# Two attention blocks with feed-forward layers on one core: the experts' weight loads grouped behind two key transposes instead of four

## The chip, the core and the metric

The kernel runs on one core of one Trainium2 chip. The metric is the device time of one execution in microseconds. Five engines work side by side: TensorE (PE, with its weight loads PEld), VectorE (DVE), ScalarE (ACT), GpSimd (POOL) and SyncE (SP), which here does nothing but issue transfers; 16 DMA engines carry them out. All semaphores and orders are written by hand.

## The reference, cut to what matters

Eight batches of 128 tokens with 128 features pass two layers. Each layer is cross-attention with 16 heads of 8 features against a shared context, followed by a feed-forward part: a quantized gated one in layer 0, eight experts with the best two mixed in layer 1.

```python
x = x + L0_xattn(layernorm(x), ctx, ctx, mask_per_batch, Wq, Wk, Wv, Wo)   # 16 heads of 8, softmax over 128 keys
x = x + L0_ffn(layernorm(x), w_gate, w_up, w_down)                         # quantized activations and weights, silu
x = x + L1_xattn(layernorm(x), ctx, ctx, shared_mask, Wq, Wk, Wv, Wo, bo)
h = relu(einsum('td,ehd->eth', xt, W1) + b1)       # the experts: E = 8, hidden 256
y = einsum('eth,eoh->eto', h, W2) + b2
out = einsum('eto,te->to', y, comb)                # comb: softmax weights of the top 2 experts
```

W1 and W2 are the experts' weights: 8 x 256 x 128 numbers of 4 bytes each, 1 MB apiece. They are used in the last part of layer 1 alone.

## The kernel before

A unit is one layer of one batch; there are 16, numbered n = 0 to 15 in the order of `UNIT_ORDER` (line 76). n = 0 to 6 are layer 0 of batches 0 to 6, n = 7 is layer 1 of batch 0, n = 8 layer 0 of batch 7. Each unit is a chain of named steps: `kv` (keys and values), `ks` (the key transpose), `q`, `max` (a first product of queries and keys for the row maxima, four parts), `qb`, `exp` (the shifted scores, four parts), `pv`, `oT`, `aT`, `wo`, and then in layer 0 the feed-forward steps `xq`, `fxT`, `gate`, `th`, `z1`, `up`, `hT`, `down`, or in layer 1 the router and the expert steps `z` and `y`.

A planner (`plan`, line 303) runs on the host before the kernel is built. It turns costs, due times and biases into one fixed order of steps for each engine; the engines then run these orders strictly, with a semaphore wait ahead of each step. The planner knows the key transposes but not the loads that are issued between them, so its orders are the same whatever loads stand there.

The keys of a unit are put by ScalarE and GpSimd into `kst`, a bf16 tile of 128 x 2048, and SyncE turns them by a DMA transpose (step `ks`, line 617) into `kblk`, which has five slots. TensorE reads `kblk` first in step `max` (lines 761 and 763: a mask matmul, then the products) and again in `exp` (line 779). `max` of n = 6 waits for the transpose of n = 6. In TensorE's order around it stand: qb of n = 4, the last part of max of n = 5, the first part of max of n = 6, exp of n = 4, fxT of batch 0, aT of n = 2, exp, the second part of max of n = 6, exp, gate of batch 0, fxT of batch 1, wo of n = 2, exp, up of batch 0, pv of n = 3. In VectorE's order z1 of batch 0 (line 1262) comes after wo of n = 2; it reads the tanh that ScalarE (line 1039) makes of the gate matmul.

SyncE issues all loads of the later phases between its transposes: after the transpose of unit n it calls `later_loads(n)` (line 578). For n = 1 these are two mask loads and half of the context. For n = 5 they begin with three small ones (b1, gT, gb). The tiles w1_sb and w2_sb are filled in four parts of four chunks each, every part two transfers of 256 KB (128 rows of 2 KB), part k behind the transpose of n = 5 + k. All eleven transfers count up one semaphore, s_moe, to 176; the logit and `z` steps of layer 1, batch 0, wait for that full count.

SyncE's order is: ks of n = 0 to 8, qs of n = 7, ks of n = 9 and so on. Each ks waits for GpSimd's last step on the keys of its unit and for the transpose two before it. All transfers issued by SyncE go through one hardware queue.

Of the kernel before, what the change touches and what calls it, by code (L numbers as in the profile page):

```python
# [378 lines left out]
def build(nc, x, ctxT, mask0, mask0T, mask1, mask1T, w0q, w0kv, w0o, w1q, w1kv, w1o, bo,  # L379
# [17 lines left out]
    with ExitStack() as ctx:  # L397
        def sb(name, shape, dt=F32):
            return ctx.enter_context(nc.sbuf_tensor(name, shape, dt))

        def sem(name):
            return ctx.enter_context(nc.semaphore(name))
# [9 lines left out]
        def after(eng, step, u, i=None):  # L412

            eng.wait_ge(done[step], u * counts[step] + (counts[step] if i is None else i + 1))
# [11 lines left out]
        def wait_landed(eng, n, name="ks"):  # L426
            eng.wait_ge(landed[name][n % 2], 16 * (n // 2 + 1))
# [24 lines left out]
        w1_sb = sb("w1_sb", [P, ZCH, P])  # L452
        w2_sb = sb("w2_sb", [P, ZCH, P])
# [64 lines left out]
        s_cst, s_x0, s_x, s_ctx0, s_ctx, s_wq, s_wkv, s_w1, s_wo, s_b2, s_moe = [sem(n + "_in") for n in (  # L518
            "cst", "x0", "x", "ctx0", "ctx", "w0q", "w0kv", "w1", "w0o", "b2", "moe")]
# [48 lines left out]
        @block.sync  # L568
        def _(sp):
            sp.dma_start(x_sb[:, 0, :], x[0]).then_inc(s_x0, 16)  # L570
            sp.dma_start(cst_sb[:, :], cst).then_inc(s_cst, 16)
            sp.dma_start(x_sb[:, 1:4, :], x[1:4].rearrange("b t d -> t b d")).then_inc(s_x, 16)
            def masks(part, first, last):
                sp.dma_start(m0_i[:, first:last, :], mask0[first:last].rearrange("b q k -> q b k")
                             ).then_inc(s_mask[2 * part], 16)
                sp.dma_start(m0T_i[:, first:last, :], mask0T[:, first:last, :]).then_inc(s_mask[2 * part + 1], 16)

            def later_loads(n):

                if n == 0:  # L580
                    masks(1, 1, 2)
                    sp.dma_start(wo_sb[0][:, :], w0o).then_inc(s_wo, 16)
                    sp.dma_start(x_sb[:, 4:NB, :], x[4:NB].rearrange("b t d -> t b d")).then_inc(s_x4, 16)
                if n == 1:
                    masks(2, 2, 4)
                    sp.dma_start(ctx_sb[:, 4:NB, :], ctxT[:, 4:NB, :]).then_inc(s_ctx4, 16)
                if n == 2:
                    masks(3, 4, NB)
                if n == 3:
                    for k, src in enumerate((wg, wu, wd)):  # L590
                        sp.dma_start(wf_sb[:, k, :], src).then_inc(s_wf[k], 16)
                if n == 4:
                    sp.dma_start(m1_i[:, :], mask1).then_inc(s_mask1[0], 16)
                    sp.dma_start(m1T_i[:, :], mask1T).then_inc(s_mask1[1], 16)
                    for dst, src in ((wq_sb[1], w1q), (wkv_sb[1], w1kv), (wo_sb[1], w1o),
                                     (bo_sb, bo.partition_broadcast(P))):
                        sp.dma_start(dst[:, :], src).then_inc(s_w1, 16)
                    sp.dma_start(b2_sb[0:3, :], mb2.partition_broadcast(3)).then_inc(s_b2, 16)
                if n == 5:
                    sp.dma_start(b1_sb[:, :], mb1).then_inc(s_moe, 16)  # L600
                    sp.dma_start(gT_sb[:, :], gT).then_inc(s_moe, 16)
                    sp.dma_start(gb_sb[:, :], gb.partition_broadcast(P)).then_inc(s_moe, 16)
                if n in (5, 6, 7, 8):
                    part = slice(4 * (n - 5), 4 * (n - 5) + 4)
                    sp.dma_start(w1_sb[:, part, :], m1T[:, part, :]).then_inc(s_moe, 16)
                    sp.dma_start(w2_sb[:, part, :], m2T[:, part, :]).then_inc(s_moe, 16)

            masks(0, 0, 1)
            for name, n, _ in order["sp"]:
                b = units[n][1]  # L610
                if name == "ks":
                    after(sp, "pool.kl", n)
                    if n >= KSLOTS:
                        after(sp, "pe.exp", n - KSLOTS)
                    if n >= 2:
                        wait_landed(sp, n - 2)
                    sp.dma_start_transpose(kblk[:, n % KSLOTS, :, :, :].rearrange("p j g k -> p (j g) k"),
                                           kst[:, n % 2, :, :, :].rearrange("p j g c -> p (j g c)")
                                           ).then_inc(landed["ks"][n % 2], 16)
                    later_loads(n)  # L620
                if name == "qs":
                    after(sp, "pool.ql", n)
                    if n >= TSLOTS:
                        after(sp, "pe.max", n - TSLOTS)
                    if b >= 2:
                        wait_landed(sp, b - 2, "qs")
                    sp.dma_start_transpose(qT[:, n % TSLOTS, :, :], qst[:, n % QSLOTS, :, :].rearrange("p g c -> p (g c)")
                                           ).then_inc(landed["qs"][b % 2], 16)
                if name == "qb":
                    after(sp, "dve.m3", n)  # L630
                    if n >= MSLOTS:
                        after(sp, "pe.exp", n - MSLOTS)
                    if b >= 2:
                        wait_landed(sp, b - 2, "qb")
                    sp.dma_start_transpose(qmT[:, n % MSLOTS, :, :], qst[:, n % QSLOTS, :, :].rearrange("p g c -> p (g c)")
                                           ).then_inc(landed["qb"][b % 2], 16)
                if name == "out":
                    if b < NB - 1:
                        after(sp, "pool.sum", b)
                    else:  # L640
                        sp.wait_ge(last_out_ready, 1)
                    sp.dma_start(out[b], out_sb[:, b % 2, :]).then_inc(s_out[b % 2], 16)
            for stored in s_out:
                sp.wait_ge(stored, 8 * NB)
# [785 lines left out]
```

## Time and profile before

| | us |
|---|---|
| median of 3 runs | 217.01 (216.96 to 217.01) |
| profiled execution | 216.0 |
| span of the profiled execution | 214.1 |

| engine | busy us | share of the span |
|---|---|---|
| TensorE matmuls | 192.9 | 90% |
| TensorE weight loads | 152.1 | 71% |
| VectorE | 173.1 | 81% |
| ScalarE | 134.9 | 63% |
| GpSimd | 86.3 | 40% |

The times of the sections below count from the start of the span. Busy shares are means over stages that differ: read a stage by its windows, and a wait by the instruction that comes next on its engine. The page also has a row of the clock that was granted to TensorE, in 40 slices of 5.35 us (9 stands for 90% or more), and one with the busy share of the DMA engines.

### The profile page before, as it was taken

To read this page: it belongs to the slowest core of one execution; us is meant where nothing else is said; L and a number is where in the kernel's file an instruction comes from. 1 tells how busy PE (TensorE), PEld (TensorE's weight loads), DVE (VectorE), ACT (ScalarE), POOL (GpSimd) and SP (SyncE) were. 2 spreads that over 40 slices of the span, in tenths; PEclk is the share of its full clock that TensorE was granted. 3 is DMA by queue.
4 is the path that set the end of the run, shared out by engine and by line. 5 is a ranking of instruction groups with operands and counts; after the bars stand their busy time and mean duration, and the time that the engine had idled before them with its cause. 6 is when DMAs were issued, how large, how long until landed. Compare 5 with 4: busy or idle time off the path is not lost.

```text
span 214.1 us, 5873 instructions
## 1 busy us (share of the span) xinstructions
PE 192.9 (90%) x1966; PEld 152.1 (71%) x1981; DVE 173.1 (81%) x625; ACT 134.9 (63%) x378; POOL 86.3 (40%) x199
## 2 busy tenths in 40 slices
PE   8789899889987779889999979999998999999992
PEld 3346477656664456566689647998897899999992
DVE  4549898889999989999998999888699817455265
ACT  3465188663886488559568767947645883475740
POOL 7887023714304573544323645343045103612450
PEclk9999999999999969999999999999999999999999
DMA  5589926459071624459574048720231100000000
GB/s 157 124 211 256 194 75 162 37 135 233 7 196 41 158 51 102 92 123 180 106 80 112 5 112 152 147 52 12 52 76 39 35 18 0 14 15 0 15 0 25
DMA packets 57987, 19.28 MB, mean 90 GB/s; under 512 B 51299, under 2 KB 56291, under 8 KB 57958
## 3 DMA queue, kind: packets, MB, share of 16 engines
q1 hardware_dynamic: 57382, 18.46, 40.3%
q10 hardware_dynamic: 576, 0.46, 0.7%
q8 instruction: 16, 0.26, 0.5%
q14 instruction: 13, 0.11, 0.2%
HBM read 5.80 MB, written 0.52 MB: 30 GB/s over the span
## 4 chain that ended last, share of the span: by engine, by line
PE 52%; DVE 22%; issue 8%; POOL 6%; ACT 4%; DMA 4%; SPq 1%; DVEq 0%; POOLq 0%; ACTq 0%
PE ps_B L928 14%; PE ps_A L941 10%; DVE mx L1179 4%; PE ps_O L853 4%; PE ps_B L779 3%; PE ps_A L761 3%; PE ps_A L763 3%; DMA kblk<-kst 2%; DVE z L1262 2%; DVE ps_B L1356 2%; PE ps_O L861 2%; PE ps_X L819 2%; PE ps_Q L795 2%; DMA m1T_i<-in_mask1T 2%; PE ps_P L833 2%
## 5 line engine op out<-in xcount | busy, mean ns | idle before, releaser
L1014 ACT ACTIVATE probs<-ps_B 128x512 f32<-128x512 f32 x64 | 37.6, 604 | 17.2 <-DVE ps_B L1356 13.6
L1179 DVE TENSOR_REDUCE mx<-ps_A 128x4 f32<-128x512 f32 x64 | 42.3, 680 | 1.3 <-PE ps_A L763 1.2
L1073 ACT ACTIVATE hid<-ps_B,b_sb 128x128 f32<-128x128 f32 x128 | 35.5, 387 | 11.7 <-PE ps_B L928 11.6
L928 PE MATMUL ps_B<-mxT,w_sb 128*128 128x128 f32 x256 | 33.4, 280 | 0.3 <-ACT probs L1014 0.2
L928 PEld LDWEIGHTS ps_B<-mxT,w_sb 128*128 128x128 f32 x256 | 30.4, 191 | 1.9 <-issue 1.3
L941 PE MATMUL ps_A<-w_sb,hid 128*128 128x128 f32 x256 | 31.1, 275 | 0.5
L941 PEld LDWEIGHTS ps_A<-w_sb,hid 128*128 128x128 f32 x256 | 31.1, 192 | 0.5
L761 PE MATMUL ps_A<-m_b,id_b 128*128 128x512 bf16 x64 | 24.4, 382 | 2.1 <-DMA kblk<-kst 0.8
L763 PE MATMUL ps_A<-kblk,qT 112*128 112x256 bf16 x128 | 24.5, 272 | 0.0
L726 POOL TENSOR_TENSOR yc<-yc 128x512 f32<-128x512 f32 (+2 forms) x21 | 17.3, 822 | 17.8 <-DVE yc L1334 16.7
L779 PE MATMUL ps_B<-qmT,kblk 118*128 118x128 bf16 x256 | 23.5, 220 | 0.5 <-ACT probs L1014 0.3
L779 PEld LDWEIGHTS ps_B<-qmT,kblk 118*128 118x128 bf16 x256 | 18.6, 98 | 5.9 <-ACT probs L1014 1.3
L654 POOL TENSOR_SCALAR hv<-mv 128x1 f32<-128x1 f32 x32 | 7.6, 236 | 37.4 <-DVE mv L1227 34.7
L1356 DVE TENSOR_TENSOR ps_B<-ps_B,limit 128x512 f32<-128x512 f32 x32 | 21.5, 689 | 0.8 <-PE ps_B L779 0.7
L696 POOL CAST kst<-kr 128x128 bf16<-128x128 f32 x32 | 9.0, 309 | 32.5 <-DVE kr L1164 32.3
L1334 DVE TENSOR_TENSOR yc<-ps_A,comb 128x512 f32<-128x512 f32 x16 | 11.0, 690 | 13.2 <-PE ps_A L941 13.0
L657 POOL TENSOR_TENSOR ry<-hv,half 128x1 f32<-128x1 f32 x32 | 18.8, 588 | 2.7
L763 PEld LDWEIGHTS ps_A<-kblk,qT 112*128 112x128 bf16 x128 | 12.6, 98 | 8.2
L853 PE MATMUL ps_O<-probs,v_sb 128*9 128x128 f32 x512 | 17.0, 273 | 1.1 <-DVE x_sb L1221 0.6
L949 ACT ACTIVATE oT_sb<-ps_O 128x512 f32<-128x512 f32 x16 | 9.6, 603 | 9.7 <-PE ps_O L853 9.7
L853 PEld LDWEIGHTS ps_O<-probs,v_sb 128*9 128x9 f32 x512 | 12.5, 90 | 4.0 <-issue 3.2
L706 POOL CAST qst<-qr 128x256 bf16<-128x256 f32 x16 | 6.6, 416 | 18.9 <-DVE qr L1172 18.9
(140 smaller groups left out, 388.3 us busy)
## 6 DMA issues: line engine op xcount, KB each, us to landing
w_sb<-in_m1T SPq DMA_DIRECT2D x4, 256.0 KB, 3.5
w_sb<-in_m2T SPq DMA_DIRECT2D x4, 256.0 KB, 4.2
out_y<-out_sb SPq DMA_DIRECT2D x8, 64.0 KB, 1.5
kblk<-kst SPq DMA_TRANSPOSE x16, 4.4
x_sb<-in_x SPq DMA_DIRECT2D x1, 256.0 KB, 2.9
ctx_sb<-in_ctxT SPq DMA_DIRECT2D x1, 256.0 KB, 3.6
m_i<-in_mask SPq DMA_DIRECT2D x1, 256.0 KB, 3.1
m0T_i<-in_mask0T SPq DMA_DIRECT2D x1, 256.0 KB, 5.0
```

The lines of the kernel that those rows point to most:

```text
L657: ends(pool.tensor_tensor(ry[:, k, b, :], hv[:, k, b, 0:1], half[:, :], ALU.pow), step)
L726: sum_part(pool.tensor_tensor(y[:, 0:w, :], y[:, 0:w, :], y[:, w:2 * w, :], ALU.add))
L761: pe.matmul(o[:, :].rearrange("p (h k) -> p h k", h=4), id_b[:, :], m, start=True, stop=False)
L763: mm = pe.matmul(o[:, 256 * (g % 2):256 * (g % 2) + 256].rearrange("p (j k) -> p j k", j=2), qT[0:ROWS, n % TSLOTS, g, :], kblk[0:ROWS, n ...
L779: mm = pe.matmul(o[:, P * (h % 4):P * (h % 4 + 1)], kblk[0:MROWS, n % KSLOTS, h % 2, h // 2, :], qmT[0:MROWS, n % MSLOTS, h // 2, :], star ...
L853: mm = pe.matmul(o[32 * j:32 * j + DH + 1, (h // 4) * P:(h // 4 + 1) * P], v_sb[:, n % KSLOTS, h, :], probs[:, n % 2, h, :], start=True, s ...
L928: mm = pe.matmul(psum("z", b, i)[:, c * P:(c + 1) * P], w1_sb[:, 4 * i + c, :], mxT[:, b % 2, :], start=True, stop=True)
L941: mm = pe.matmul(o[:, e * P:(e + 1) * P], hid[:, b % 2, c, :], w2_sb[:, c, :], start=False, stop=(c == 8 * i + 7))
L1014: ends(act.activation(probs[:, n % 2, 4 * i:4 * i + 4, :], psum("exp", n, i)[:, :].rearrange("p (h k) -> p h k", h=4), ACT.Exp, scale=ATTN ...
L1073: ins = act.activation(hid[:, b % 2, 4 * i + c, :], psum("z", b, i)[:, c * P:(c + 1) * P], ACT.Relu, bias=b1_sb[:, 4 * i + c:4 * i + c + 1])
L1179: ends(dve.tensor_reduce(mx[:, n % 2, 4 * i:4 * i + 4], psum("max", n, i)[:, :].rearrange("p (h k) -> p h k", h=4), AX.X, ALU.max), "dve.max")
L1356: ends(dve.tensor_tensor(o, o, limit[:, :].unsqueeze(1).broadcast_to([P, 4, P]), ALU.min), "dve.pm")
```

## The change

The second to fourth parts of the experts' weights are issued at other places of SyncE's order. Before, one part (two transfers) follows each of the transposes of n = 5, 6, 7 and 8. After, three parts (six transfers) follow that of n = 5, and the fourth follows that of n = 6. The transfers themselves, their sizes and destinations, the semaphore and its count, and the orders of all engines are the same.

```diff
-                if n in (5, 6, 7, 8):
-                    part = slice(4 * (n - 5), 4 * (n - 5) + 4)
-                    sp.dma_start(w1_sb[:, part, :], m1T[:, part, :]).then_inc(s_moe, 16)
-                    sp.dma_start(w2_sb[:, part, :], m2T[:, part, :]).then_inc(s_moe, 16)
+                if n in (5, 6):
+                    for first in ((0, 4, 8), (12,))[n - 5]:
+                        part = slice(first, first + 4)
+                        sp.dma_start(w1_sb[:, part, :], m1T[:, part, :]).then_inc(s_moe, 16)
+                        sp.dma_start(w2_sb[:, part, :], m2T[:, part, :]).then_inc(s_moe, 16)
```

## Rows read from the trace of the kernel before

**Rows 1.** The page: the span, and the granted clock in 40 slices.

```profile
span 214.1 us, 5873 instructions
...
PEclk9999999999999969999999999999999999999999
```

**Rows 2.** Expert weights: duration min/median/max in ns, first and last start; landing.

```profile
L928 PE MATMUL ps_B<-mxT,w_sb x256: 273/275/377, 108.7 to 205.9; 128*128 128x128 f32 x128
...
L605 SPq DMA_DIRECT2D w_sb<-in_m1T x4: 432/578/586, 45.4 to 69.1; - x4
...
DMA to landing us min/median/max: 3.3/3.9/4.4
```

**Rows 3.** Windows: busy us by engine (PE, PEld, DVE, ACT, POOL), PEclk, DMA share, GB/s.

```profile
26.00:27.00 1.00, 1.00 (x14) 0.83 (x12) 0.60 (x1) 0.15 (x1) 0.00 (x0) 1.00 1.02 385
...
53.00:56.00 3.00, 2.79 (x26) 1.93 (x26) 2.90 (x15) 2.57 (x8) 0.00 (x0) 1.00 0.15 57
56.00:60.00 4.00, 3.79 (x56) 3.07 (x57) 4.00 (x15) 3.30 (x7) 1.72 (x5) 1.00 0.31 71
60.00:64.00 4.00, 3.39 (x36) 2.39 (x38) 4.00 (x19) 3.55 (x10) 0.00 (x0) 1.00 0.69 191
...
72.00:76.00 4.00, 2.30 (x11) 1.17 (x9) 4.00 (x27) 2.19 (x7) 2.25 (x6) 1.00 0.27 94
76.00:80.00 4.00, 3.22 (x21) 2.29 (x23) 3.41 (x21) 3.26 (x9) 3.56 (x9) 0.58 0.21 48
```

**Rows 4.** Timeline of SyncE: start us, duration us, what is issued.

```profile
15.24 2.92 SPq L617 DMA_TRANSPOSE kblk<-kst  x1
...
45.45 0.43 SPq L605 DMA_DIRECT2D w_sb<-in_m1T  x1
45.92 0.43 SPq L606 DMA_DIRECT2D w_sb<-in_m2T  x1
47.15 2.67 SPq L617 DMA_TRANSPOSE kblk<-kst  x1
...
57.78 1.60 SPq L617 DMA_TRANSPOSE kblk<-kst  x1
```

**Rows 5.** Landing, us from issue: those issued at 45.45, 45.92, 47.15, 57.78.

```profile
w_sb<-in_m1T SPq DMA_DIRECT2D x1, 256.0 KB, 3.5
...
w_sb<-in_m2T SPq DMA_DIRECT2D x1, 256.0 KB, 4.1
...
kblk<-kst SPq DMA_TRANSPOSE x1, 4.8
...
kblk<-kst SPq DMA_TRANSPOSE x1, 3.6
```

**Rows 6.** DMA packets, windows 16.5:17, 17:17.5, 46.75:47.75, 51.25:52.25, 52.25:53.25, 59:60, 60:61.

```profile
DMA packets 75, 0.13 MB, mean 252 GB/s; under 512 B 5, under 2 KB 22, under 8 KB 75
...
DMA packets 292, 0.16 MB, mean 312 GB/s; under 512 B 244, under 2 KB 246, under 8 KB 292
...
DMA packets 221, 0.22 MB, mean 220 GB/s; under 512 B 115, under 2 KB 115, under 8 KB 221
...
DMA packets 130, 0.19 MB, mean 189 GB/s; under 512 B 41, under 2 KB 41, under 8 KB 130
...
DMA packets 137, 0.25 MB, mean 252 GB/s; under 512 B 14, under 2 KB 14, under 8 KB 137
...
DMA packets 1095, 0.28 MB, mean 280 GB/s; under 512 B 1095, under 2 KB 1095, under 8 KB 1095
...
DMA packets 993, 0.29 MB, mean 286 GB/s; under 512 B 971, under 2 KB 971, under 8 KB 993
```

**Rows 7.** Timeline of TensorE: the first matmul of max, n = 6.

```profile
53.04 0.38 PE L761 MATMUL ps_A<-m_b,id_b 128*128 128x512 bf16 x1
```

**Rows 8.** Timeline of ScalarE and VectorE: the tanh and z1 of batch 0.

```profile
56.47 0.69 ACT L1039 ACTIVATE wf_sb<-ps_A,fs 128x512 f32<-128x512 f32 x1
...
57.36 0.65 DVE L1262 SCALAR_TENSOR_TENSOR z<-wf_sb,ps_A 128x512 f32<-128x512 f32 x1
```

## The prediction

> **What bounds the kernel now.** I took the time first: one profiled execution of 216.0 us, of which 214.1 us are the span and 1.9 us lie around it [rows 1]; the median of the three timed runs, 217.01 us, is 1.01 us above the profiled one. The sums below are made against 216.0 and carried to the median by adding 1.01.
>
> Then I asked who uses the moved data. The expert weights are first read by TensorE at 108.6 us [rows 2], while the last load of W1 is issued at 69.1 us, that of W2 right behind it, and none of the eight takes over 4.4 us to land [rows 2]. So the loads have over 30 us to spare, nobody waits for them, and the change can't gain by bringing them earlier. What counts is what stands behind them in SyncE's queue.
>
> Third, the windows by engine around the place of the change. From 53 to 56 us TensorE is busy 2.79 of 3.00 us and VectorE 2.90; from 56 to 64 VectorE is busy all of 8.00 us and TensorE 7.18 [rows 3]. Two engines run side by side without slack, each in a fixed order: TensorE can't go round a step that has to wait, and once VectorE loses time there, nothing later in this stretch gives it back.
>
> Fourth, SyncE's own timeline [rows 4] and the landing times [rows 5]. The sixth key transpose is followed by one pair of 256 KB loads, issued at 45.45 and 45.92 us. The seventh transpose (n = 6) is issued right after, at 47.15, and lands 4.8 us later, at 51.95. The next, issued at 57.78 with nothing ahead of it, takes 3.6 us. The seventh is the tight one: TensorE's first matmul on it, the mask matmul that opens max of n = 6, starts at 53.04 [rows 7], after a landing at 51.95. That is a slack of 1.09 us. The eighth and ninth are not tight: in TensorE's order their first matmuls stand behind the feed-forward blocks 0 to 3, far later than 60 us.
>
> **The change part by part.**
>
> *Removed: two pairs of loads, behind n = 7 and n = 8.* Two issues each, of 0.43 to 0.59 us [rows 2], leave SyncE behind the transpose of 57.78 and behind the next one, where SyncE has nothing else due for several us, and no engine waits for these transfers. Gain taken: 0. Should the data in motion slow an engine's accesses, the gain would be a little over 0; VectorE and TensorE work through 56 to 64 at 8.00 and 7.18 us of 8.00 with the loads beside them [rows 3], which leaves little to win.
>
> *Added: two pairs of loads behind n = 5, ahead of the transpose of n = 6.* First the queue. The two loads there are issued 0.47 us apart [rows 4], so four more end the batch at about 48.3 us (45.92 + 5 × 0.47) instead of 46.4. The transpose, which now starts at 47.15, is pushed to 48.3, by 1.15 us. With an unchanged 4.8 us it would land at 53.1 us, 0.06 us after it is wanted. The issue alone thus uses up the slack and costs next to nothing.
>
> Then the data. The question is whether a transpose waits for the data of loads issued ahead of it. The trace has such a case. The transpose issued at 15.24 us stands behind three loads. In 16.5 to 17.0 us only 5 packets under 512 B (the form a transpose's data has) moved among 75; in 17.0 to 17.5 there were 244 of 292 [rows 6]. Its data began about 1.8 us after its issue, and the one issued at 57.78 began by 59.0, about 1.2 us after. So the queue drains roughly in order, loads first. The Trainium skill ("DMA: Bandwidth & Descriptors", Queues, rings and completion order) says the same more sharply: each DMA engine consumes descriptors in ring order, and the increment that reports completion lands only after every earlier write of that engine. By that rule the transpose can't be reported before the last load on any engine is written; the trace agrees, and the sum is the same with or without it.
>
> Then the rate at which these loads drain. The first pair landed at 48.95 and 50.02 (45.45 + 3.5, 45.92 + 4.1) [rows 4, 5], 1.07 us apart. The packets of 2 KB and over (all less those under 2 KB; 128 of them make one load) are 106 in 46.75 to 47.75, 89 in 51.25 to 52.25, and 123 in 52.25 to 53.25 [rows 6]: 1.21, 1.44 and 1.04 us for a load. I take 1.1 us, between the landing gap and the best of these rates, since a longer batch has fewer starts and tails. The ends are 1.44 us, and at the fast side the rate at which transposes move, 280 GB/s [rows 6], which is 0.94 us for 262144 B, and the best rate of the whole trace, 385 GB/s in 26 to 27 us [rows 3], which is 0.68.
>
> The working: data of the batch starts at 46.75, 1.3 us after the first issue. Six loads at 1.1 us end at 53.35. The transpose's data then takes 2.1 us (59.0 to about 61.1, where only 22 packets of 2 KB had followed before 61 [rows 6]), and it lands 0.3 us after its last data (57.78 + 3.6 = 61.4 against 61.1). That gives 55.75 us, 3.8 us later than now. The issue doesn't delay it further, since at the 2.67 us that it takes now [rows 4] it is over by 51.0, before its data can move.
>
> Then who waits. TensorE stands at 53.04 and goes on at 55.75: 2.7 us in which everything behind in its order waits too: the exp scores of n = 4, the transposes and gate and up matmuls of the first feed-forward blocks, wo of n = 2. VectorE has some work in hand and sees less of that at first. But the step z1 at 57.36 needs ScalarE's tanh, which ends at 56.47 + 0.69 = 57.16 [rows 8] and depends on the gate matmul in the delayed part of TensorE's order. Its slack is 0.2 us. So VectorE loses 2.7 − 0.2 = 2.5 us by z1, and from there to 76 us it has no idle time to pay it back from. Every later step hangs on these two engines, so the end moves by 2.5 us.
>
> *The fourth part, behind n = 6.* One pair stays, as now, behind a transpose that is itself later. It moves at about 56 to 58.5, and the next transpose comes at 57.78 + 2.5. Cost 0: nobody waits for it either.
>
> Sum: 216.0 + 2.5 = 218.5 profiled, 219.5 us as a median.
>
> **The rivals.**
>
> *The clock falls too (B).* TensorE was busy only 2.30 of 4.00 us in 72 to 76, and in 76 to 80 the granted clock was 0.58 on average, that is 3.4 us at 1.2 GHz instead of 2.4 [rows 3]; it is the only dip after the start [rows 1]. A standstill of 2.7 us may bring another. Against it: TensorE is nearly full on both sides of the standstill, and it was not in 72 to 76. Price: 3.4 us at half rate loses 1.7 us of TensorE's work, and its idle time in 56 to 64 is 0.8 us, so 0.9 to 1.7, taken as 1.2. Time 219.5 + 1.2 = 220.7.
>
> *A dense batch (C).* Six loads in a row may move at 280 GB/s, as nothing shows whether a pair is limited by its start. At 0.94 us they end at 52.4, the transpose lands at 54.8, TensorE stands 1.75 us, VectorE loses 1.55: 218.6.
>
> *The slow side (F).* At 1.44 us a load they end at 55.4, the transpose lands at 57.8, TensorE stands 4.8 us: 221.6.
>
> *The loads don't hold the transpose (D).* If the batch moves as fast as 0.68 us a load, it ends at 50.8 and the transpose lands at 53.2, 0.2 us late, which VectorE's slack takes. The same comes out if the transpose's data passes that of the loads: landing 53.1. Then nothing is lost: 217.0. The case at 15.24 us speaks against the passing, and all three packet rates against the speed. The Trainium skill ("DMA: Bandwidth & Descriptors", Specifications) gives about 358 GB/s as what one core gets from HBM, which would be 0.73 us a load, a landing at 53.55 and 217.3 us by this sum, an estimate from that page; these loads have not come near it in any window of rows 6.
>
> *Faster (E).* Case D has to hold, and the shift of a few tenths must also take away the dip at 76 to 80. VectorE is busy 3.41 of 4.00 us there [rows 3]; without the dip it could win at most those 0.6 us: 216.4. It decides from the point where the transpose lands before 53.04 + 0.2 and TensorE has more to do in 72 to 76. Nothing in the change gives it more to do there, which is why it gets little. That the change doesn't do what it says isn't a case: the loads are plain instructions of SyncE and nothing reorders them.
>
> **How the numbers follow.** The forecast (A, 219.5) 0.48; B (220.7) 0.20; C (218.6) 0.12; D (217.0) 0.11; E (216.4) 0.05; F (221.6 and over) 0.04. A measurement of this kernel can tell about 0.2% (0.43 us) from no change. Slower by over 0.2%: A, B, C and F, 0.84. Within it: D, 0.11. Faster: E, 0.05. The range holds A, B and C with the rounding of B's price, 217.4 to 221.9, and leaves out D, E and F, 0.20.
>
> **What would show it.** SyncE's timeline: six issues of weights from 45.45, and the transpose of n = 6 near 48.3. Its landing: 55 to 56 us (C 54.8, D 53.2, F 57.8). Among TensorE's waits a new line, the mask matmul of line 761 waiting for kblk, of 2.7 us; VectorE idle for over 2 us in all up to z1. Granted clock 1.00 in 55 to 62 for A, a second dip there for B. The steps behind 58 us shifted by an equal 2.5 us up to the end. The prediction is wrong if the transpose lands by 53.2, or if it lands near 56 and the shift at 76 us or at the end is much under 2.5 us: then there was slack downstream that I don't see.

## The result, and the profile after

| | us |
|---|---|
| changed kernel, median of 4 runs | 221.38 (220.12 to 222.19) |
| kernel before, beside it | 216.99 |
| ratio | 1.020, 95% interval 1.015 to 1.025 |
| profiled execution | 222.19 |
| span of the profiled execution | 220.3 |

The change makes the kernel 2.0% slower, 4.4 us by the medians; the two profiled executions lie 6.2 us apart. The change adds a line, so line numbers from 605 on are one higher than in the kernel before (in the experiments with further edits, a few more).

The page of the changed kernel: the share of the engines and the granted clock in 40 slices, now of 5.5 us.

```profile
span 220.3 us, 5873 instructions
...
PE 195.8 (89%) x1966; PEld 154.0 (70%) x1981; DVE 173.5 (79%) x625; ACT 134.9 (61%) x378; POOL 86.0 (39%) x199
...
PEclk9999999999699985999999999999999999999999
```

The work of VectorE, ScalarE and GpSimd is the same to 0.4 us, and that of TensorE is 2.9 us more for the same instructions: part of them ran at a lower clock. Where the kernel before had one dip of the clock [rows 1], there are two.

SyncE's timeline (start, duration, what is issued), to be held against [rows 4]:

```profile
45.54 0.43 SPq L606 DMA_DIRECT2D w_sb<-in_m1T  x1
...
47.91 0.43 SPq L607 DMA_DIRECT2D w_sb<-in_m2T  x1
48.46 6.02 SPq L618 DMA_TRANSPOSE kblk<-kst  x1
54.52 0.58 SPq L606 DMA_DIRECT2D w_sb<-in_m1T  x1
```

The transpose of n = 6 goes out 1.3 us later, and its issue holds SyncE for 6.02 us instead of 2.67. The landing, in us from issue, of the last of the six loads and of this transpose:

```profile
w_sb<-in_m2T SPq DMA_DIRECT2D x1, 256.0 KB, 6.7
...
kblk<-kst SPq DMA_TRANSPOSE x1, 8.2
```

So the last load lands at 54.6 and the transpose at 56.7 (48.46 + 8.2), 4.7 us later than the 51.95 of [rows 5]. TensorE's timeline (in brackets the idle time before it and what ended it) shows what it meets. The same matmul started at 53.04 in [rows 7].

```profile
52.96 0.38 PE L764 MATMUL ps_A<-kblk,qT 112*128 112x256 bf16 x2
56.76 0.57 PE L762 MATMUL ps_A<-m_b,id_b 128*128 128x512 bf16 x1 [3.41 <-issue]
57.12 0.64 PE L764 MATMUL ps_A<-kblk,qT 112*128 112x256 bf16 x2
```

It stands for 3.4 us. The profile names no releaser and writes "issue"; the landing at 56.7 is what tells it. VectorE, in its own timeline, then waits three times, 4.4 us in all, and reaches z1 at 62.35, which was 57.36 in [rows 8]:

```profile
57.79 0.69 DVE L1180 TENSOR_REDUCE mx<-ps_A 128x4 f32<-128x512 f32 x1 [2.62 <-PE ps_A L764]
59.73 0.23 DVE L1258 TENSOR_SCALAR xq<-xr 128x128 bf16<-128x128 f32 x1 [1.24 <-ACT xr L1050]
60.54 0.69 DVE L1180 TENSOR_REDUCE mx<-ps_A 128x4 f32<-128x512 f32 x1 [0.58 <-PE ps_A L764]
...
62.35 0.69 DVE L1263 SCALAR_TENSOR_TENSOR z<-wf_sb,ps_A 128x512 f32<-128x512 f32 x1
```

The windows (columns as in [rows 3]) place the clock:

```profile
53.00:56.00 3.00, 0.35 (x3) 0.06 (x1) 2.09 (x13) 0.83 (x2) 0.00 (x0) 1.00 1.17 282
56.00:60.00 4.00, 3.24 (x16) 2.00 (x17) 0.92 (x2) 1.24 (x4) 0.00 (x0) 0.60 0.53 132
60.00:64.00 4.00, 3.90 (x58) 2.88 (x58) 3.44 (x12) 3.20 (x8) 1.71 (x5) 0.97 0.04 9
...
80.00:84.00 4.00, 2.83 (x19) 2.05 (x19) 3.62 (x22) 2.92 (x7) 2.62 (x7) 0.59 0.01 4
84.00:88.00 4.00, 3.78 (x27) 2.80 (x27) 2.19 (x10) 2.98 (x8) 1.43 (x5) 0.56 0.82 187
```

A granted 0.60 over 4 us and 0.97 over the next are 3.4 us at 1.2 GHz instead of 2.4 (2 × 0.40 × 4 + 2 × 0.03 × 4). This is a new dip, directly behind the stand. The second is the old one of 76 to 80 us, shifted, and twice as long in this pair of executions: 6.8 us at 1.2 GHz instead of 3.4. The last section shows that the kernel before has the long one too, in about half of its executions.

The shift grows in three steps. At the end of the stand it is 3.7 us (56.76 against 53.04), at z1 it is 5.0 (62.35 against 57.36), and it stays there up to the second dip. VectorE's instructions on either side of that dip, two of the kernel before and then the same two of the changed one:

```profile
74.94 0.28 DVE L1221 TENSOR_TENSOR x_sb<-ps_O,x_sb 128x128 f32<-128x128 f32 x1
...
80.82 0.35 DVE L1291 SCALAR_TENSOR_TENSOR x_sb<-ps_X,fs,x_sb 128x128 f32<-128x128 f32 x1 [0.54 <-PE ps_X L908]
...
79.97 0.28 DVE L1222 TENSOR_TENSOR x_sb<-ps_O,x_sb 128x128 f32<-128x128 f32 x1
...
86.81 0.35 DVE L1292 SCALAR_TENSOR_TENSOR x_sb<-ps_X,fs,x_sb 128x128 f32<-128x128 f32 x1 [1.15 <-PE ps_X L909]
```

The shift is 5.0 us ahead of the second dip and 6.0 behind it, and it ends at 6.2: the first result is stored at 128.49 us instead of 122.30. So the stand, the first dip and the longer second dip cost 3.7, 1.3 and 1.2 us in this execution.

### The profile page after: what moved, and what is told of

It is laid out like the page before. It is cut to its first block, busy times and chain, and to the rows that moved or that the text cites. A ratio compares the mean times of both kernels' runs of the same rounds, so it can differ in the third digit from the quotient of the medians.

```text
span 220.3 us, 5873 instructions
## 1 busy us (share of the span) xinstructions
PE 195.8 (89%) x1966; PEld 154.0 (70%) x1981; DVE 173.5 (79%) x625; ACT 134.9 (61%) x378; POOL 86.0 (39%) x199
## 4 chain that ended last, share of the span: by engine, by line
PE 53%; DVE 19%; issue 9%; POOL 6%; DMA 5%; ACT 5%; SPq 1%; ACTq 0%; DVEq 0%; POOLq 0%
PE ps_B L929 13%; PE ps_A L942 10%; PE ps_B L780 4%; PE ps_O L854 4%; PE ps_A L762 4%; DVE mx L1180 4%; PE ps_A L764 3%; DMA kblk<-kst 2%; PE ps_B L777 2%; DVE ps_B L1357 2%; PE ps_O L862 2%; PE ps_X L820 2%; PE ps_Q L796 2%; PE ps_P L834 2%; DMA m1T_i<-in_mask1T 2%
## 5 line engine op out<-in xcount | busy, mean ns | idle before, releaser
L1015 ACT ACTIVATE probs<-ps_B 128x512 f32<-128x512 f32 x64 | 37.6, 605 | 22.4 <-DVE ps_B L1357 13.6
L762 PE MATMUL ps_A<-m_b,id_b 128*128 128x512 bf16 x64 | 24.9, 389 | 5.5 <-issue 3.4
L780 PE MATMUL ps_B<-qmT,kblk 118*128 118x128 bf16 x256 | 24.5, 227 | 0.5 <-ACT probs L1015 0.3
L780 PEld LDWEIGHTS ps_B<-qmT,kblk 118*128 118x128 bf16 x256 | 19.4, 102 | 6.6 <-issue 1.4
```

The lines of the kernel that those rows point to most:

```text
L762: pe.matmul(o[:, :].rearrange("p (h k) -> p h k", h=4), id_b[:, :], m, start=True, stop=False)
L780: mm = pe.matmul(o[:, P * (h % 4):P * (h % 4 + 1)], kblk[0:MROWS, n % KSLOTS, h % 2, h // 2, :], qmT[0:MROWS, n % MSLOTS, h // 2, :], star ...
L1015: ends(act.activation(probs[:, n % 2, 4 * i:4 * i + 4, :], psum("exp", n, i)[:, :].rearrange("p (h k) -> p h k", h=4), ACT.Exp, scale=ATTN ...
```

## The experiments

Theory Q: the transpose of n = 6 waits for the data of the loads queued ahead of it, TensorE stands for it, and the clock falls behind the stand. The rivals are the issue time on SyncE alone (I), a cost of a long batch wherever it stands (S), and a clock that costs nothing beyond the stand. All ratios are against runs of the kernel before on the same chip, whose times lay between 214.5 and 217.6 us.

**One part behind n = 5, three behind n = 6.**

```diff
-                    for first in ((0, 4, 8), (12,))[n - 5]:
+                    for first in ((0,), (4, 8, 12))[n - 5]:
```

> One part (two loads) stays behind the transpose of n = 5, the other three parts (six loads) go behind that of n = 6. Theory Q (the transpose of n = 6 waits for the data of the loads queued ahead of it, and only that transpose is wanted early): it has two loads ahead as before, lands about 4.8 us after its issue, and the next transpose is not wanted before 80 us, so 217.0 us, same as before. Rival S (a long batch of loads costs by its own, by crowding memory and the DMA engines, wherever it stands): the stretch 50 to 58 us slows and the time is 1 us or more above 217.0.

Measured: ratio 0.998 (0.994 to 1.002). The same batch of six, one place further on, costs nothing. The transpose of n = 6 lands 4.2 us after its issue, TensorE doesn't stand, and z1 comes 16.4 us after the transpose of n = 5 is issued, as in the kernel before (57.62 − 41.25; 57.36 − 40.99). So theory S, a cost of a long batch wherever it stands, falls.

**All eight behind n = 6.** `((), (0, 4, 8, 12))` in the same line.

> All eight expert loads behind the transpose of n = 6, none behind n = 5. Theory Q: this transpose has nothing ahead of it, lands 3.6 to 3.8 us after its issue at 47.2, 1 us before the landing of the kernel before, which nobody can use, since TensorE reaches its first matmul on it at 53.0 either way: 1.000 of before. Rival (the landing sets TensorE's pace there even in the kernel before): TensorE's max of n = 6 starts earlier, 0.3 to 1 us less.

Measured: ratio 0.999 (0.997 to 1.002). The transpose lands after 3.7 us instead of 4.8, and nothing is won: in the kernel before this landing was already early enough.

**Two parts behind each.** `((0, 4), (8, 12))` in the same line.

> Two parts (four loads) behind n = 5, two behind n = 6. Theory Q: two loads less ahead of the transpose of n = 6 than in the changed kernel. There six loads held it to a landing at 56.7; at 1.1 to 1.2 us for each load four loads give a landing near 54.3, TensorE stands about 1.3 us, the step z1 of batch 0 is 1.1 us late, and without a clock dip the time is 218.1. With a dip 219.3. Rival I (the issue time on SyncE alone delays it): the transpose is issued 0.5 us late and lands at 52.9: 217.0.

Measured: ratio 1.007 (1.004 to 1.010), 1.5 us. The transpose is issued at 46.40 and lands 6.9 us later, at 53.3 and so 1 us earlier than expected, and TensorE stands for 0.97 us:

```profile
kblk<-kst SPq DMA_TRANSPOSE x1, 6.9
...
53.43 0.38 PE L762 MATMUL ps_A<-m_b,id_b 128*128 128x512 bf16 x1 [0.97 <-issue]
```

The granted clock of 56 to 60 us is 1.00 here: this stand of 1 us brings no dip. From issue to landing the transpose takes 3.7 us (no pair ahead), 4.8 (one, kernel before), 6.9 (two) and 8.2 (three), and with more pairs ahead it is also issued later. What stays the same is its distance from the loads: in all nine profiles where it is issued behind one, two or three full pairs still under way in its own queue, and none on another, it lands 1.9 to 2.1 us after the last of these loads (51.95 against 50.02 in the kernel before, 56.66 against 54.61 in the changed one). This is the plainest sign of theory Q.

**The issues alone.** Four of the six loads behind n = 5 move 16 rows of 128; the rest follows later.

```diff
+                if n == 5:
+                    for first in (8, 12):
+                        part = slice(first, first + 4)
+                        sp.dma_start(w1_sb[0:16, part, :], m1T[0:16, part, :]).then_inc(s_moe, 16)
+                        sp.dma_start(w2_sb[0:16, part, :], m2T[0:16, part, :]).then_inc(s_moe, 16)
```

> Behind n = 5 stand six issues as in the changed kernel, but four of them move only 16 of the 128 rows (32 KB instead of 256); the other 112 rows follow behind n = 7 and n = 8 (the count of the semaphore is adapted). Theory I (SyncE's issue time delays the transpose): it is issued at 48.4 as in the changed kernel and the time is that of the changed kernel, about 221. Theory Q (the data ahead delays it): four loads with 128 KB in all add about 0.5 us of data, the issue comes 1.2 us late, landing at 53 to 53.5, a stand of 0 to 0.5 us: 217.0 to 217.5.

Measured: ratio 1.002 (1.000 to 1.005). SyncE issues the transpose at 48.01, nearly as late as in the changed kernel, and it lands 4.6 us later, at 52.6, before TensorE reaches it at 52.8. Theory I falls: the slack takes the time of four issues, and the data is what costs.

**TensorE kept at work through the stand.** The changed kernel with 15 matmuls of zeros ahead of the wait.

```diff
+                if n == 6 and i == 0:
+                    wait_free(pe, "max", n, i)
+                    for _ in range(15):
+                        pe.matmul(psum("max", n, i)[:, :].rearrange("p (h k) -> p h k", h=4), fill_b[:, :],
+                                  fill_b[:, :].unsqueeze(1).broadcast_to([P, 4, P]), start=True, stop=True)
```

> The changed kernel with 15 extra matmuls of zeros on TensorE (0.21 us each, into the bank that max of n = 6 overwrites next) ahead of the wait for the transpose of n = 6, so that TensorE works through the 3.4 us in which it stands now. Theory K (3.7 us are the stand itself, and the rest of the 4.4 us of the median and 6.2 us of the profile comes from the clock granted after it): granted clock 1.00 in 53 to 61 us, z1 of batch 0 at 61.1 instead of 62.4, and the time 1.2 us or more below the changed kernel's 221.4, at 219.8 to 220.2. Rival: the clock costs nothing beyond the stand (VectorE bounds): 221.4.

Measured: ratio 1.018 (1.009 to 1.026). The first dip is gone:

```profile
56.00:60.00 4.00, 3.88 (x52) 2.71 (x53) 2.84 (x11) 3.40 (x9) 0.96 (x3) 1.00 0.25 89
```

z1 comes 19.7 us after the transpose of n = 5 is issued (59.94 − 40.22), against 21.2 in the changed kernel (62.35 − 41.13) and 16.4 before. Part of the 1.5 us is the stand, which ended 0.3 us later in the changed kernel's profile. The dip alone is seen from the mask matmul of max of n = 6 to z1: 5.6 us with it (62.35 − 56.76), 4.4 without it (59.94 − 55.52), 4.3 before. So it makes z1 1.2 us late, and the stand makes it 3.3 to 3.7 us late. The time doesn't settle whether that reaches the end, as the interval is wider than the difference, and the ratio is above the 1.013 to 1.015 that was expected. The fill itself costs a little: the transpose lands at 55.1, and the zeros hold TensorE to 55.5. The second dip is still there.

**The kernel before with TensorE kept at work in 73 to 76 us.** Five matmuls of zeros in its gaps ahead of the dip that [rows 3] show at 76 us.

```diff
+                late = {("aT", 5): 2, ("wo", 5): 1, ("q", 7): 2}.get((name, n), 0)
+                if late:
+                    wait_free(pe, "gate", 4)
+                for _ in range(late):
+                    pe.matmul(psum("gate", 4)[:, :].rearrange("p (h k) -> p h k", h=4), fill_b[:, :],
+                              fill_b[:, :].unsqueeze(1).broadcast_to([P, 4, P]), start=True, stop=True)
```

> The kernel before with five extra matmuls of zeros on TensorE in its idle gaps at 73 to 76 us (two ahead of aT of n = 5, one ahead of its wo, two ahead of q of n = 7; into a free bank of ring A). If the fall of the clock to half at 76.8 comes from TensorE's idling in 72 to 76 and costs time on the path: granted clock 1.00 in 76 to 80 and up to 0.6 us less, 0.997 of before. Rival: VectorE bounds there and nothing is won, or the fill itself delays aT and q: 1.000 to 1.002.

Measured: ratio 0.992 (0.990 to 0.995), faster than the kernel before by 1.6 us where 0.6 was expected at most. TensorE's busy time in 72 to 76 goes from 2.30 to 3.23 us, the clock stays up through the whole page, and VectorE is busy through 80 to 84, where it was busy 3.46 us of 4 before (the last of these lines is of the kernel before):

```profile
PEclk9999999999999999999999999999999999999999
```

```profile
72.00:76.00 4.00, 3.23 (x20) 1.59 (x20) 4.00 (x28) 2.67 (x8) 2.21 (x6) 1.00 0.15 58
76.00:80.00 4.00, 3.28 (x33) 2.15 (x33) 3.84 (x20) 3.70 (x9) 3.65 (x10) 1.00 0.31 70
80.00:84.00 4.00, 3.64 (x54) 2.46 (x53) 4.00 (x14) 3.53 (x10) 1.37 (x4) 1.00 0.60 135
...
80.00:84.00 4.00, 3.68 (x37) 2.54 (x34) 3.46 (x9) 3.74 (x9) 1.84 (x5) 0.99 0.69 156
```

**The changed kernel with both fills, and with the late one alone.**

> The changed kernel with both fills: 15 matmuls ahead of the wait of max of n = 6 and five in 78 to 81 us. Theory K: with neither dip what is left is the stand of 3.3 us, so 1.015 of before. If the second dip stays, 1.018 as with the first fill alone.

> The changed kernel with the five late matmuls alone (in 78 to 81 us), none in the stand. With e7 (both fills, 1.009 of before) this gives the price of the first dip by itself, the one behind the stand. By the trace z1 of batch 0 was 1.5 us later with that dip than without it; if this is carried to the end, the ratio is 1.009 + 0.007 = 1.016. If it is lost downstream, 1.009 to 1.011.

Measured: 1.009 (1.007 to 1.011) with both, 1.015 (1.010 to 1.019) with the late one alone. The page of the first shows no dip, that of the second shows one, at the stand, and a short fall at the very end of the span. With both fills the kernel is better than the 1.015 that was expected: that sum took the stand alone against the kernel before, which has a dip of its own that is gone here. Of the run with the late fill alone:

```profile
56.63 0.59 PE L762 MATMUL ps_A<-m_b,id_b 128*128 128x512 bf16 x1 [3.43 <-issue]
```

**The changed kernel again, beside these.**

> The changed kernel unchanged, beside the two above on the same chip, as their reference: 1.020 of before, a stand near 3.4 us before max of n = 6, two dips of the clock.

Measured: 1.022 (1.016 to 1.027). Its stand is 2.6 us in the profiled execution and the first dip is there.

These make a table of prices, as differences of ratios times 216.4 us. The last column is what the 95% intervals of the two ratios leave open.

| what | from | us | within |
|---|---|---|---|
| the stand | 1.0091 / 0.9924 (both fills / kernel before with the late fill) | 3.6 | 0.6 |
| the first dip | 1.0146 − 1.0091; 1.0219 − 1.0177 | 1.2; 0.9 | 1.0; 2.2 |
| the second dip, in the changed kernel | 1.0219 − 1.0146; 1.0177 − 1.0091 | 1.6; 1.9 | 1.5; 1.9 |
| the second dip, in the kernel before | 1 − 0.9924 | 1.6 | 0.5 |

The stand and the first dip make up the change: 3.6 + 1.1 = 4.7 us, where 4.4 were measured at first and 4.7 in the repetition. This is not an independent check, since the ratios of the table form a chain from one kernel to the other; it says that the second dip costs both about the same, and the intervals leave 1.5 us open there. The stand and the second dip of the kernel before are clear of the noise, and the first dip only just. The traces give it more sharply: from the mask matmul to z1 it takes 5.3 to 5.6 us in the three profiles of the changed kernel with the dip, and 4.4 in the two without. So the first dip costs 0.9 to 1.2 us at z1, and from z1 to the second dip no profile gives any of it back.

**The four extra loads on ScalarE's queue.** Parts 2 and 3 are issued by ScalarE behind its last step on the keys of n = 7.

```diff
+                    if n == 7:
+                        for first in (4, 8):
+                            part = slice(first, first + 4)
+                            act.dma_start(w1_sb[:, part, :], m1T[:, part, :]).then_inc(s_moe, 16)
+                            act.dma_start(w2_sb[:, part, :], m2T[:, part, :]).then_inc(s_moe, 16)
```

> As the changed kernel, but the second and third parts (four loads) are issued on ScalarE's own queue, behind its last step on the keys of n = 7, at 47.7 to 49.6 us, where ScalarE idles for 3.2 us. SyncE issues one pair behind n = 5, so its transpose of n = 6 goes out at 47.2. Theory Q in its strict form (only what is ahead in the same queue holds the transpose): landing near 52, no stand, 217.0. Rival S (the 16 DMA engines are shared, and 1 MB in flight beside the transpose takes its share of them): 524 KB of transpose beside 1 MB of loads that together move at 230 to 290 GB/s, landing at 53.5 to 55, a stand of 0.5 to 2 us, 217.3 to 218.8.

Measured: ratio 1.045 (1.042 to 1.047). This is far worse than either theory gave. The transpose is issued at 46.97, when one of ScalarE's four loads is out (46.92, 47.29, 47.77 and 48.34), and lands 13.6 us later, 0.3 us after the last of them (60.57 against 60.24); TensorE stands for 7.7 us. The landing, the window of 53 to 56 us and TensorE's timeline:

```profile
kblk<-kst SPq DMA_TRANSPOSE x1, 13.6
...
53.00:56.00 3.00, 0.02 (x1) 0.00 (x0) 1.76 (x10) 0.51 (x2) 0.00 (x0) 1.00 1.17 127
...
60.71 0.59 PE L762 MATMUL ps_A<-m_b,id_b 128*128 128x512 bf16 x1 [7.68 <-issue]
```

So the strict form of theory Q falls: it isn't only the order within one queue that holds the transpose, and another queue is no way around. In 53 to 56 us the DMA engines were fully busy with only 127 GB/s moved; why two queues side by side move so little is open. The Trainium skill ("DMA: Bandwidth & Descriptors", Rules for kernel authors) says that spreading transfers over SyncE, ScalarE and GpSimd doesn't help, since they interleave on the same 16 engines; the run agrees, and shows that it can harm: it is 2.5% slower than the changed kernel (1.045 against 1.020).

**Is there something better still?** All eight loads behind n = 6, with the late fill.

> All eight expert loads behind the transpose of n = 6, with the five late matmuls: is there a version better than the kernel before with the late matmuls (0.9924 of before)? If the place of the loads is free on this side, the same 0.992; if the earlier landing of the transpose of n = 6 gives anything once the clock stays up, below 0.990.

Measured: ratio 0.993 (0.989 to 0.996), within the noise the same as with the loads where they were. The clock is what there was to win; the place of the loads isn't.

**Does the transpose slow the loads ahead of it?** In the changed kernel the six loads move fast, then at about 100 GB/s for 2.5 us, then at up to 392. The packets of 49 to 51 us, and the DMA share and GB/s in 48.5 to 51 us (last two numbers of the second line):

```profile
DMA packets 107, 0.20 MB, mean 100 GB/s; under 512 B 9, under 2 KB 9, under 8 KB 107
```

```profile
48.50:51.00 2.50, 2.23 (x42) 1.48 (x41) 2.50 (x11) 0.00 (x0) 2.00 (x6) 1.00 0.93 108
```

The engines are busy 0.93 of that time with little to show. The last run lets SyncE issue the transpose only once the six loads have landed.

```diff
+                    if n == 6:
+                        sp.wait_ge(s_moe, 144)
                     sp.dma_start_transpose(kblk[:, n % KSLOTS, :, :, :].rearrange("p j g k -> p (j g) k"),
```

> The changed kernel, but SyncE issues the transpose of n = 6 only when all nine transfers behind n = 5 have landed. In every run with the transpose issued beside four or six loads (changed kernel, two pairs, both fills) the load data falls to about 100 GB/s for 2.5 us from the moment the transpose is issued, with the DMA engines busy; in the run with six loads and no transpose beside them it kept about 300 GB/s. Theory T (the issue of a transpose beside loads in flight slows these loads): now the six loads move without that spell, the last lands at 52.2 to 52.8 instead of 54.6, and the transpose, issued then, lands 3.7 us later at 56.0 to 56.6, so about the changed kernel's time although it waits longest: 1.020. Theory R (the loads are slow by themselves there): the last load lands at 54.6 as before, the transpose at 58.4, the stand grows to 5.3 us, ratio 1.030.

Measured: ratio 1.032 (1.028 to 1.037). The last load lands 6.0 us after its issue instead of 6.7, at 53.4; the transpose is issued then, takes 4.5 us, and TensorE stands for 5.0:

```profile
53.43 1.61 SPq L620 DMA_TRANSPOSE kblk<-kst  x1
...
kblk<-kst SPq DMA_TRANSPOSE x1, 4.5
...
58.00 0.59 PE L764 MATMUL ps_A<-m_b,id_b 128*128 128x512 bf16 x1 [5.00 <-issue]
```

Without the transpose beside them the loads are through 0.5 to 0.9 us sooner (6.0 us for the last one, against 6.5 to 6.9 in the five profiles with it). The rest of the slow spell is there without it, in a milder form. So theory R nearly holds, theory T is right for a small part at most, and what slows the loads in 49 to 51 us stays open. The same six loads behind the transpose of n = 6 had no such spell in 51.5 to 54.5 us: they moved at 291 to 315 GB/s.

## Why the prediction was right, and where its sizes were off

**That the loads bring nothing by coming earlier.** Right: the runs with six or eight loads behind n = 6 are within 0.2% of before.

**The place.** Right: the transpose of n = 6 is the one with little slack, and the wait appears at the mask matmul of max of n = 6. The same loads one place later are free.

**The issue time, 1.15 us, absorbed by the slack.** Right: 48.46 against the 48.3 of the sum, and 1.002 for the issues alone. The issue itself took 6.02 us where the sum took 2.67; it changed nothing, as SyncE had nothing else due, and because the data ahead was the later of the two.

**The rate of the loads, 1.1 us each.** As a mean a little low. The last of the 2 KB packets move at about 54.0, which is 7.2 us for six from 46.75 and so 1.2 us each: 0.6 us. That the mean came out so near is partly luck, as no steady rate lies behind it: the loads of the batch landed 2.0, 1.8, 0.7, 0.7 and 0.8 us apart. The end of the batch moved at the rate of case D, and the slow spell at its start, for which the sum had no term, made up for it. The tail from the last data to the landing was taken as 0.3 us from an undisturbed transpose, and was 0.7. Landing 56.7 instead of 55.75, and a stand of 3.4 us instead of 2.7.

**The slack at z1, 0.2 us, and no payback.** No payback is right: VectorE's shift stays within 0.1 us from z1 up to the second dip in every profile of the changed kernel, and the stand's price is 3.6 us at the end by the run with both fills. The slack wasn't there: z1 came 4.4 us after the mask matmul of max of n = 6 in the profiles with a late transpose and no dip (two pairs; both with the stand filled), against 4.3 before, so the delay went through whole. The sum had 2.5 us.

**The clock.** This is the step that failed in its weight. Case B had 0.20, since TensorE was nearly full on both sides of the stand. That argument carried nothing: the clock fell to 1.2 GHz in the last 0.5 us of the stand or right at its end in every profile of the changed kernel that left it unfilled, the one with the late fill among them (three of three, stands of 2.6 to 3.4 us), not after one of 0.97 us, and never where the stand was filled. Its price was taken as 1.2 us, and was 0.9 to 1.2 by the ratios and by the traces at z1, and 1.3 by the first pair of profiles.

So 219.5 came from the right mechanism with two terms too small: the stand by 1.1 us and the clock by 1.1. The measured 221.38 is within the range because that reached to case B. B's own 220.7 would have been nearer.

**The dip at 76 us as a gain of at most 0.6 us (case E).** Too small: taking it away won 1.6 us on the median. Two things are in that. For the 3.4 us dip of the profiled execution the traces give 0.8: the run with the late fill is 0.5 us ahead of the kernel before up to 75 us and 1.4 ahead from 93 on. The 0.6 us was VectorE's idle time in 76 to 80 alone, but VectorE also idled 0.54 us in 80 to 84. The rest is the longer dip that many other executions have (see below). A dip has to be priced by how much later the work behind it runs, and not by the bounding engine's idle time inside it, and over several executions.

## What to carry to other kernels

A load that nobody waits for is still not free of place: ask which transfer is queued behind it, when that is wanted, and how many bytes stand ahead, since here the data ahead in the queue, and not the time of the issues, decided. Moving the loads behind the urgent transfer was free; moving two of the three parts to another engine's queue made the kernel 4.5% slower. Where TensorE stands for a few us, expect a spell at half clock on top, about 1 us here, and try to fill the gaps ahead of a known dip with matmuls on zeros if a bank is free: that won 0.8% here, more than any place of the loads.

## What the runs showed of the hardware

**The clock's dips come in two lengths.** In the eleven profiles that have dips, each of them amounts to 3.4 us or to 6.8 us at 1.2 GHz by its windows (a fall at the very end, where TensorE runs out of work, left aside). The one at the stand is 3.4 us with stands of 2.6 to 3.4 us, and 6.8 with those of 5.0 and 7.7. It begins 2.1 to 3.8 us after TensorE's last matmul, so in the longest stand most of it, 3.9 us, passes while TensorE does nothing. The kernel before had 3.4 us [rows 3]; one part behind n = 5 and three behind n = 6 had 6.8, as these windows give (2 × 0.14 × 4 + 4 + 2 × 0.21 × 4 = 6.8):

```profile
72.00:76.00 4.00, 2.48 (x11) 1.42 (x12) 4.00 (x25) 1.92 (x7) 2.52 (x6) 0.86 0.00 0
76.00:80.00 4.00, 3.57 (x22) 2.48 (x23) 3.58 (x21) 2.96 (x7) 3.29 (x9) 0.50 0.12 28
80.00:84.00 4.00, 3.96 (x35) 2.92 (x34) 2.28 (x8) 3.39 (x9) 0.88 (x3) 0.79 0.78 177
```

That execution took 217.17 us, while the same kernel's median is 215.39. This fits the scatter of the kernel before, 214.5 to 217.6 us, and of the changed one, 219.5 to 222.2; with the late fill the former has 214.1 to 215.3. The mean granted clock that is recorded with every execution bears it out. It is 0.983 or 0.984 in the profiled executions whose one dip is long, and 0.989 to 0.991 in those with one short dip. Of the 62 further executions of the kernel before, 32 have 0.982 to 0.984, 26 have 0.989 to 0.992 and 4 have 0.996; with the mean of their chip taken off, the first are 0.7 us longer than the second, and these 0.7 us longer than the four. So a large part of the scatter goes with the dip's length, and the short dip of the profile before was not the usual case. What makes a dip short or long wasn't tested.

**The issue of a transpose lasts until the loads ahead of it have all but landed.** SyncE is held for 1.6 us by a transpose with nothing ahead, 2.1 to 2.7 with one pair of loads, 4.9 with two and 5.7 to 6.3 with three. In the nine profiles with full pairs under way ahead in its queue alone, the issue ends 0.05 to 0.4 us before the last of them lands (54.48 against 54.61 in the changed kernel). Nothing else can go out on SyncE meanwhile; here nothing else was due.

**A transpose and loads of two queues hurt each other.** 1 MB of loads on ScalarE's queue beside one transpose of 512 KB raised its landing from 4.8 to 13.6 us, while the same bytes ahead of it in its own queue raised it to 8.2.

**The rate of a load isn't a constant of its size.** The same 256 KB loads moved at 100 GB/s in 49 to 51 us, at 373 to 392 in 52 to 53.5, and at 291 to 315, by windows of 1 us, behind the transpose in the run with three parts behind n = 6. The cause is open.
